# Head attention: the scores of a step ahead of the values, and the four heads' transposes in one piece

## The reference, cut to what matters

```python
h = relu(layernorm(x)); x = x + three_graph_convolutions(h, adj)      # layer 0
h = relu(layernorm(x)); x = x + additive_attention(h, adj)            # layer 1
h = relu(layernorm(x)); x = x + head_attention(h, adj)                # layer 2, the change is here
h = relu(layernorm(x)); x = x + normalised_convolution(h, adj)        # layer 3

def head_attention(x, adj):                     # 4 heads of 32 columns
    Q, K, V = x @ Wq + bq, x @ Wk + bk, x @ Wv + bv
    scores = Q_h @ K_h.T / sqrt(32) + (1 - adj) * -1e9        # 2048 x 2048 for each head
    return concat_h(softmax(scores) @ V_h) @ Wo + bo
```

## Time and profile before

| | |
|---|---|
| median of 3 runs | 12629.11 us |
| the profiled execution | 12638.63 us, span 12636.8 us |
| granted TensorE clock | 0.991 of full speed over the span |
| TensorE matmul busy | 12330.1 us, 98% |
| VectorE busy | 9716.8 us, 77% |
| ScalarE busy | 9594.3 us, 76% |
| GpSimd busy | 420.5 us, 3% |

### The profile page before, as it was taken

One profiled execution on the slowest core, in us unless ns is written; L12 is line 12 of the kernel. 1 busy time (PEld: TensorE's weight loads), 2 busy tenths in 40 slices (PEclk: granted clock), 3 DMA queues, 4 the chain that ended last, 5 costly groups with the idle time before them and its releaser, 6 DMA issues.

```text
span 12636.8 us, 250099 instructions
## 1 busy us (share of the span) xinstructions
PE 12330.1 (98%) x109953; PEld 6057.6 (48%) x109953; DVE 9716.8 (77%) x13670; ACT 9594.3 (76%) x8545; POOL 420.5 (3%) x636
## 2 busy tenths in 40 slices
PE   7999999999999999999999999999999999999999
PEld 3333843338433384333843338433484334843348
DVE  4888848888488885888758887588875888758887
ACT  3888748887488874888749887488874888748886
POOL 1000000000000000000000000000000000000000
PEclk9999999999999999999999999999999999999999
DMA  2000320003200031000310003100031000310003
GB/s 76 18 21 18 104 79 21 18 18 110 76 18 18 18 118 68 18 18 21 125 59 18 18 22 130 53 18 18 23 137 45 18 18 26 138 40 18 21 24 106
DMA packets 205754, 610.39 MB, mean 48 GB/s; under 512 B 45057, under 2 KB 136833, under 8 KB 139137
## 3 DMA queue, kind: packets, MB, share of 16 engines
q1 hardware_dynamic: 183792, 450.72, 10.4%
q0 software_dynamic: 20880, 143.66, 3.1%
HBM read 556.47 MB, written 8.39 MB: 45 GB/s over the span
## 4 chain that ended last, share of the span: by engine, by line
PE 91%; DVE 7%; SPq 1%; DMA 1%; issue 1%; ACT 0%; POOL 0%; DVEq 0%
PE ps L1235 53%; PE ps L1217 10%; PE ps L1319 7%; PE ps L1332 4%; PE ps L1248 4%; PE ps L1392 4%; PE ps L1299 3%; PE ps L1167 2%; PE ps L1378 2%; DVE E L790 1%; DVE E L791 1%; DVE PT L817 1%; PE ps L1200 1%; DVE E L792 1%; DVE T L913 1%
## 5 line engine op out<-in xcount | busy, mean ns | idle before, releaser
L1235 PE MATMUL ps<-E,a_win 128*32 128x512 f32 x65536 | 7134.3, 594 | 48.2 <-DVE E L792 36.9
L1235 PEld LDWEIGHTS ps<-E,a_win 128*32 128x32 f32 x65536 | 2111.7, 110 | 4872.2 <-issue 4726.9
L558 ACT ACTIVATE E<-Q,ka 128x2048 f32<-128x2048 f32 x2048 | 4074.6, 1990 | 0.0
L790 DVE TENSOR_SCALAR E<-Q,kd 128x2048 f32<-128x2048 f32 x2048 | 2631.4, 1285 | 989.4 <-PE ps L1235 963.7
L557 ACT ACTIVATE E<-Q,ka 128x1280 f32<-128x1280 f32 x2048 | 2786.6, 1361 | 791.2 <-PE ps L1235 767.4
L791 DVE TENSOR_SCALAR E<-Q,kd 128x2048 f32<-128x2048 f32 x2048 | 2632.0, 1285 | 0.0
L792 DVE TENSOR_SCALAR E<-Q,kd 128x768 f32<-128x768 f32 x2048 | 1263.3, 617 | 0.0
L913 DVE CUSTOM_DVE_ANT_0 T<-ps,adj_ring 128x2048 f32<-128x2048 f32 x512 | 1172.1, 2289 | 88.5 <-PE ps L1299 85.4
L589 ACT ACTIVATE T<-T,nmin 128x2048 f32<-128x2048 f32 x512 | 1028.1, 2008 | 217.6 <-DVE nmin L913 217.6
L1319 PE MATMUL ps<-ident,T 128*128 128x128 f32 x8192 | 1098.6, 276 | 16.5 <-DVE HT L875 12.3
L1319 PEld LDWEIGHTS ps<-ident,T 128*128 128x128 f32 x8192 | 913.1, 141 | 198.1 <-ACT PT L471 71.4
(11 more groups left out here) (131 smaller groups left out, 7588.1 us busy)
## 6 DMA issues: line engine op xcount, KB each, us to landing
adj_ring<-in_adj SPq DMA_DIRECT2D x384, 1024.0 KB, 5.1
adj_res<-in_adj POOLq DMA_DIRECT2D x128, 1024.0 KB, 7.0
qcur<-AGG SPq DMA_DIRECT2D x896, 16.0 KB, 2.8
qcur<-HT SPq DMA_DIRECT2D x896, 16.0 KB, 2.2
HW<-in_x POOLq DMA_DIRECT2D x9, 1024.0 KB, 7.4
X<-in_x SPq DMA_DIRECT2D x128, 64.0 KB, 1.9
out_x<-X SPq DMA_DIRECT2D x8, 1024.0 KB, 17.2
wq_r<-in_L_gnn_Wq SPq DMA_DIRECT2D x4, 64.0 KB, 2.5
```

Of the source, the lines that this page charges most:

```text
L558: nc.scalar.activation(E[:, s + 3, :], Q2[:, :], ACT.Relu, bias=ka[:, u, 48 + m:49 + m]).then_inc(e_act, 1)
L790: nc.vector.tensor_scalar(E[:, s, :], Q2[:, :], kd[:, u, m:m + 1], 0.0, ALU.add, ALU.max)
L1235: last = mm(ps[QROWS * grp:QROWS * (grp + 1), 4 * u + c, :], win, E[:, s + grp, c * CH:(c + 1) * CH], start=(m == 0), stop=(m == QUADS - 1 ...
```

## The change

Two lists are written in another order; no instruction is added or taken away. On TensorE the values V of a step stand behind its scores S, and not between T2 and T3. On VectorE the small copy `values_out` (L937), which takes the finished values of a tile out of bank 3 once per tile, stands behind `min2` of its step.

```diff
             def step2(b, s):                       # vector block
...
-                if r == 1 and 0 <= t - 2 < NT:
-                    values_out(b, t - 2)
                 if 0 <= s - 5 < GROUPS:
                     evac2(b, s - 5)
...
                 if s < STEPS:
                     min2(b, s)
+                if r == 1 and 0 <= t - 2 < NT:
+                    values_out(b, t - 2)

             def step2(b, s):                       # tensor block
...
                     for h in range(HEADS - 1):
                         probs_t2(b, q, h)
-                if 0 <= q - 1 < GROUPS:
-                    values2(b, q - 1)
                 if 0 <= q < GROUPS:
                     probs_t2(b, q, HEADS - 1)
...
                 if s < STEPS:
                     scores2(b, s)
+                if 0 <= q - 1 < GROUPS:
+                    values2(b, q - 1)
```

## The result

| | before | after |
|---|---|---|
| median | 12629.69 us (9 runs, 12627.6 to 12632.39) | 12664.82 us (9 runs, 12660.3 to 12674.55) |
| profiled execution, span | 12636.8 us | 12663.4 us |

The ratio is 1.0029, 95% interval 1.0020 to 1.0037. The forecast was 12664 us.

What follows compares the result with a forecast made beforehand. TensorE's chain, 15.65 us a tile, bounds the kernel. Per batch 6.6 us added less 2.2 us back, times 8, is 35 us: 12674 us profiled, median 9.5 us below, 12664 us; 8-in-10 range 12625 to 12700 us.

Steps and rivals of the forecast that it cites:

- What bounds the kernel: Head attention: 91% of the waits are TensorE, 15.65 us a tile, with 0.93 us of slips a batch.
- The change of the array: Between full width and 32-column strips: same count before and after, scores to values taken at 0.09 us; cost nothing.
- What it adds: Head attention: T3, R and O wait for ScalarE's copies of T0 and T1, together 6.6 us a batch.
- O "likewise": In tiles, O waits for ScalarE's copy of T1 as R does, 0.11 us each.
- What it gives back: Slips 0.9 us and TensorE's waits for VectorE in the drain behind the last scores 1.3 us: 2.2 us a batch.
- The slips: A batch's first tiles: T1 and T2 wait for VectorE's late T3 copy; values ahead give room, 0.9 us back.
- The sum: Per batch 6.6 us added less 2.2 us back, net 4.4 us; times 8 batches 35 us.
- The layers around keep their lists: Layers 0, 1 and 3 keep their instruction lists; the sum gave them no cost or gain.
- the hidden change into strips: Scores to values: the scores' slot hides the strips' load, 42 us come off, some lost; 12632 us, chance 0.14.
- the dearer one: Scores to values: the change into strips costs 0.20 us, 51 us more, less some slips; 12710 us, chance 0.12.
- the copies in time: T3 and R find their banks free, nothing is added, 2.2 us a batch given back; 12611 us, chance 0.10.

Runs made afterwards that it cites:

- short copies: Changed kernel, but ScalarE copies only 256 of 512 columns of T0 and T1, and the values read those twice: 12623.53 us, 41 us below the changed kernel.
- old drain: Changed kernel with the order of before from step 64 on (values between T2 and T3, values_out ahead of evac2): 12682.55 us, 18 us above the changed kernel.
- new drain: The changed order from step 64 on (values behind all 16 transposes, values_out behind evac2); put alone into the kernel before: 12616.55 us, ratio 0.9991.
- eight kernels with the same idle stretch: Before, changed and six variants of their orders, all with 2.27 us idle ahead of layer 3's first product: 12616.55 to 12821.67 us.

## Why the prediction was right

**What bounds the kernel:** TensorE's chain, 15.65 us a tile plus slips. Held.

**The change of the array:** one into strips and one out, before and after; scores to values at the price of transposes to values. Held (values 1.01 us in both chains, and the short copies' 1.90 + 1.01 + 0.93 us). The Trainium skill's rule that a change of tiling mode drains TensorE ("TensorEngine Tiling (Array Packing)", section Key Properties) fits: joining the transposes saved nothing. In the chain the price isn't one number: 0.15 us from strips into transposes, 0.21 us into scores.

**What it adds:** T3 waits for ScalarE, 0.04 us with one wait and 0.10 us with two; measured 0.03 and 0.09 us in the chain. R 0.11 us; measured 0.11. O "likewise" 0.11 us; measured 0.17 us. O is two matmuls in the trace, and the second is late too: it starts 0.18 us behind the first, where before it was 0.11 us. That is 0.06 us x 15 x 8 = 7 us too little. The scores' 0.01 us a step are another 4 to 5 us.

**What it gives back:** the drain 1.3 us a batch; measured 1.2 us in the changed kernel and 0.8 us in the kernel before. The sum left out that the drain's T3 waits for ScalarE (0.40 us in the changed kernel). The slips 0.9 us a batch: the size came out, 0.8 us from step 12 to 60, since the 16.15 us tiles have room for them, but the reason was only half right. T1 and T2 did wait for VectorE's copy of T3 before, and the values now cover that wait. The short copies show the slips again with that cover in place, as scores that wait for the minimum. What takes them away in the changed kernel is the longer tile.

**The sum:** 35 us, and the medians differ by 35.1 us. That the two agree so closely is partly luck, as the stretches of the profiled executions show.

- Steps 12 to 60: by the sum's terms 12 tiles of 0.44 us less 0.9 us of slips, 35 us in 8 batches. Measured are 42.0 us, 7 above: O and the scores' 0.01 us are 10 us more, T3's waits 4 us less, and the slips gave 1 us less back.
- Step 60 to the last values: one tile's 0.44 us less 1.3 us, a gain of 7 us. Measured is a loss of 3.2 us. With the old drain this stretch loses 1.6 us a batch, and the new drain gives 1.2 us of it back.
- Everything else: the sum has 7 us for the two tiles left of its 15, and nothing for the other layers. Measured are -18.6 us, of which the clock in layer 3 is 11.4 us. "The layers around keep their lists" was taken to mean that they keep their time.

So the profiled execution should have come out at 12674 us and took 12665.17 us. The median was forecast 9.5 us below that, by the distance that the one profiled execution of before had from its median; the one of after lies 0.4 us from its own. The forecast of 12664 us meets 12664.82 us because these errors and that distance cancel. The clock's part isn't a property of the change: eight kernels with the same idle stretch have 0 to 8 falls.

**The rivals:** the hidden change into strips and the dearer one are both refuted by the 0.09 us between scores and values, the copies in time by the transposes, R and O of the changed kernel's chain, which came back to their old times when the copies were short.

A better kernel came out of it: the order of before in the steps with scores, the changed order in the drain, and R ahead of the last values, 12605.07 us, 0.18% below before.

## What to carry to other kernels

When a producer and the consumer of its freed buffer are moved closer together, work out what is left between them: here 0.87 us of transposes against 0.60 us of copy and two handovers, which misses by 0.03 us, and by 0.09 us where a second wait is attached (0.87 us is eight slots of 0.109 us). An order that loses in the steady steps can win in the drain, where other waits rule, so decide the two apart. Before an edit is credited with what an untouched stage gains or loses, look at the granted clock there: an idle stretch that sometimes lets it fall is better shortened than argued about.

## What the runs showed of the hardware

- From column strips back to full width costs 0.15 us in the chain ahead of a transpose and 0.21 us ahead of a 512-column float32r matmul; the weight load is idle for 0.20 us in both. Into strips it costs 0.09 us behind either (from start to start 0.202 against 0.109 us behind transposes, 0.326 against 0.235 us behind scores).
- A TensorE instruction with one wait starts its weight load 0.05 us behind the end of the copy it waits for, one with two waits 0.11 us behind the earlier trace rows. At the distances of this pipeline the wait of T3 goes by it from 0.03 to 0.09 us.
- ScalarE's copies of 512 columns last 0.60 us each but follow each other every 0.49 us.
- 2.27 us without a matmul were followed by a fall to the lower clock level in 31 of 64 cases, 1.4 us in none of 32 (only 9 of these lay where the other kernels' falls came, so these 9 are the evidence); each fall cost 1.63 us.
